# Four places in the order of one weighted cross attention stage, moved on TensorE, ScalarE, VectorE and GpSimd

## What is computed

```python
scores = jnp.einsum('bhqd,bhkd->bhqk', q, k) / jnp.sqrt(jnp.float32(d))   # 16 heads of 8
scores = scores * attention_weights            # (64, 16, 128, 77), read from memory
scores = jnp.where(attention_mask, -jnp.inf, scores)
p_attn = jax.nn.softmax(scores, axis=-1)
out = jnp.einsum('bhqk,bhkd->bhqd', p_attn, v)
out = out.transpose(0, 2, 1, 3).reshape(B, Nq, D) @ Wo.T + bo
x = queries + out                              # then layer norm, gamma, beta
```

## Time and profile before

| what | value |
|---|---|
| time, median of 3 runs | 2415.65 us (2414.92 to 2417.21) |
| time of the profiled execution | 2419.09 us |
| its span | 2417.3 us |
| granted TensorE clock, mean | 0.981 |
| busy, whole span: PE, DVE, ACT, POOL | 93%, 77%, 62%, 65% |
| A1, in the trace | from about 505 to 910 us |

### The profile page before, as it was taken

How to read it: one execution, slowest core, us unless ns; L and a number is a source line. 1 busy time by engine, 2 the same in 40 slices (tenths; PEclk the granted TensorE clock), 3 DMA queues, 4 the chain that set the end, 5 groups by cost and what they waited for, 6 DMA issues and landing times.

```text
span 2417.3 us, 90082 instructions
## 1 busy us (share of the span) xinstructions
PE 2249.4 (93%) x30214; PEld 1876.4 (78%) x30214; DVE 1862.4 (77%) x4063; ACT 1495.6 (62%) x3472; POOL 1567.2 (65%) x2374
## 2 busy tenths in 40 slices
PE   7999999978888888999999989999999999999799
PEld 5777778966666666777778968888888888888688
DVE  4888881159999996777775678899999999998465
ACT  5888885558888886888885524444444444444343
POOL 2666663139999994666667766666666666666333
PEclk9999999979999998999999989999999999999999
DMA  4111112245555542222221223333333333333121
GB/s 131 45 44 44 45 49 66 68 121 166 169 167 168 164 138 49 52 51 51 51 55 55 68 74 92 95 96 96 96 96 96 97 96 97 95 96 95 53 63 54
DMA packets 443731, 211.95 MB, mean 88 GB/s; under 512 B 206704, under 2 KB 434545, under 8 KB 443505
## 3 DMA queue, kind: packets, MB, share of 16 engines
q1 hardware_dynamic: 443632, 210.69, 32.5%
HBM read 113.54 MB, written 29.88 MB: 59 GB/s over the span
## 4 chain that ended last, share of the span: by engine, by line
PE 55%; POOL 16%; issue 12%; SPq 8%; DVE 4%; ACT 3%; DMA 1%; POOLq 0%; DVEq 0%; ACTq 0%
PE bank L1179 6%; PE bank L1453 6%; PE bank L701 5%; PE bank L1540 5%; PE bank L661 5%; PE bank L1193 4%; POOL sb_region L1038 4%; PE bank L721 3%; POOL sb_rstd L1055 3%; PE bank L1493 3%; SPq L1399 3%; SPq L1402 3%; POOL sb_z L1059 3%; PE bank L1479 2%; PE bank L1517 2%
## 5 line engine op out<-in xcount | busy, mean ns | idle before, releaser
L1739 POOL TENSOR_TENSOR sb_pn<-sb_l,sb_r_all 128x512 f32<-128x512 f32 x128 | 134.8, 1053 | 269.7 <-DVE sb_r_all L1670 228.0
L892 DVE TENSOR_REDUCE sb_max<-bank 128x8 f32<-128x616 f32 x256 | 203.3, 794 | 136.6 <-PE bank L675 69.5
L701 PE MATMUL bank<-sb_ident,sb_region 128*77 128x128 f32 x2048 | 274.5, 277 | 33.5 <-ACT sb_pT L798 32.2
L785 ACT ACTIVATE sb_region<-sb_region 128x616 f32<-128x616 f32 x384 | 276.0, 719 | 22.3 <-POOL sb_region L1038 20.8
L798 ACT ACTIVATE sb_pT<-bank 77x1024 f32<-77x1024 f32 x256 | 261.0, 1020 | 41.9 <-PE bank L701 41.8
L701 PEld LDWEIGHTS bank<-sb_ident,sb_region 128*77 128x77 f32 x2048 | 236.7, 152 | 62.1 <-issue 42.5
L897 DVE TENSOR_TENSOR sb_region<-bank,sb_max 128x616 f32<-128x616 f32 x256 | 204.6, 799 | 18.3
L721 PE MATMUL bank<-sb_pT,sb_v 77*32 77x128 f32 x6144 | 208.8, 276 | 2.8 <-ACT sb_pT L798 2.1
L721 PEld LDWEIGHTS bank<-sb_pT,sb_v 77*32 77x32 f32 x6144 | 155.6, 109 | 71.2 <-issue 65.1
L661 PE MATMUL bank<-sb_region,sb_qT 32*128 32x308 f32 x1536 | 158.8, 483 | 54.5 <-ACT sb_region L813 21.8
L1595 ACT ACTIVATE sb_oT<-bank 128x512 f32<-128x512 f32 x128 | 76.5, 598 | 213.9 <-PE bank L1507 213.9
(11 more groups left out here) (186 smaller groups left out, 6455.9 us busy)
## 6 DMA issues: line engine op xcount, KB each, us to landing
sb_region<-in_side SPq DMA_DIRECT2D x64, 616.0 KB, 3.8
sb_pT<-sb_region SPq DMA_DIRECT2D x512, 64.0 KB, 2.0
sb_kF<-sb_region SPq DMA_DIRECT2D x512, 64.0 KB, 2.1
scratch_after_A<-sb_y SPq DMA_DIRECT2D x256, 64.0 KB, 1.7
sb_fx<-scratch_after_A SPq DMA_DIRECT2D x96, 128.0 KB, 2.1
sb_mask<-in_mask SPq DMA_DIRECT2D x64, 154.0 KB, 2.3
sb_x<-scratch_after_F SPq DMA_DIRECT2D x128, 64.0 KB, 1.9
sb_ctx<-in_ctxT SPq DMA_DIRECT2D x192, 38.5 KB, 1.9
```

The source lines that it names most:

```text
L701: mm = nc.tensor.transpose(two[0:C, h * T:(h + 1) * T], p_s[b.par][:, head * C:(head + 1) * C], ident[:])
L785: nc.scalar.activation(half(p_s[b.par], k), half(p_s[b.par], k), ACT.Exp, scale=SCALE[ph]).then_inc(exp_made.sem(b), 1)
L892: nc.vector.tensor_reduce(dst, by_bank_and_head(scores_half(k)), AX.X, ALU.max).then_inc(max_made.sem(b), 1)
```

## The change

It changes only the order of calls within a step, in A1 only; A0 and A2 keep theirs. Nothing is computed otherwise, and no instruction or transfer is added or removed. On PE `attend(b-1, 1)` goes behind `transpose_p(b, 0)`. On ACT `keep_oT(b-2)` goes ahead of `keep_att(b-1)`. On DVE `peak_masked(b+1, 0)` goes ahead of `invert(b-1)`. On POOL `shift(b+1, 0)` goes ahead of `centre(b-3)`.

```diff
@@ PE, step
                 if has(-1):
                     attend(b + -1, 0, b + 2 if has(2) else None)
+                if has(-1) and ph != "A1":
                     attend(b + -1, 1)
                 if has(-2) and ph != "A0":
                     transpose_o(b + -2)
                 if has(0):
                     transpose_p(b, 0)
+                if has(-1) and ph == "A1":
+                    attend(b + -1, 1)
                 if has(-1):
                     back(b + -1)
@@ ACT, step
                 weighted = ph == "A1"
+                if has(-2) and weighted:
+                    keep_oT(b + -2)
                 if has(-1):
                     keep_att(b + -1)
-                if has(-2) and ph != "A0":
+                if has(-2) and ph == "A2":
                     keep_oT(b + -2)
@@ DVE, step_weighted
                 if has(1):
                     mask(b + 1, 0)
-                if has(-1):
-                    invert(b + -1)
                 if has(1):
                     peak_masked(b + 1, 0)
                 if has(-1):
+                    invert(b + -1)
                     normalise(b + -1)
@@ POOL, step
                     if has(-1):
                         residual(b + -1)
+                    if has(1):
+                        shift(b + 1, 0)
                     if has(-3):
                         centre(b + -3)
-                    if has(1):
-                        shift(b + 1, 0)
                     if has(-3):
                         affine(b + -3)
```

## The result

The changed kernel takes 2461.80 us (median of 3 runs, 2454.57 to 2462.11) against 2415.65 us: ratio 1.0186, 95% interval 1.0164 to 1.0209, 46 us more. The forecast was 2468 us, in a range of 2450 to 2478. The profiled execution took 2461.80 us; its span is 2460.0 us against 2417.3.

The account below looks back on a forecast made before the run. POOL with DVE's data was taken to set A1's 6.13 us step; a new loop of 4.79 + 0.28 + 0.13 + 1.00 + 0.80 = 7.00 us would add 52 us to 2415.65, giving 2468 us, range 2450 to 2478.

Parts of the forecast that it names:

- The loop and its place: In A1, last exponent, transposes, second attend, copy and ACT's step form a closed cycle of 7.00 us, against 6.13.
- Its links: Five parts of A1's new step: ACT's work 4.79, copy 0.28, wait 0.13, transposes to attend 1.00, attend to copy 0.80 us.
- exponent end to the start of the transposes: Wait in A1 between ACT's last exponent and PE's transposes of P, taken as 0.13 us.
- attend to copy: In A1, from the second attend's start on PE to its copy's start on ACT: 0.80 us, other bound 0.71.
- 0.2 us short of mattering: PE's other path, keep_q through scores and attend to transposes: 1.65 us, against 1.84 for the exponent's path.
- The ends: First copy in A1 late by 1 us; about 12 steps outside the program loop take back some 2 us.
- The other moves cost and bring nothing: In A1, reordering DVE, POOL and ACT was to have no effect; DVE and POOL have 1.2 us to spare.
- the only real gain: keep_oT ahead of the copy on ACT fills 0.16 to 0.28 us of its wait, already counted in the sum.
- The first rival: POOL stays A1's bound and its new order removes its idle time: 20 us less, 2396 us; chance 0.04.
- The shorter loop: Rival: every part of A1's closed cycle at its lower bound, 6.70 us a step, 35 us more, 2451 us.
- that rival: TensorE's clock falls in A1, lengthening each step by some 1.4 us: 85 us more, 2553 us; chance 0.02.
- The change does nothing: Rival: ACT's 0.47 us wait in A1 absorbs the new path, time within 0.2%, 2411 to 2420 us; chance 0.02.

Follow-up runs that it names:

- the order with the masks together: Kernel before, with DVE's mask of half 1 moved directly behind the mask of half 0: 2401.25 us, ratio 0.9949.

## Why the prediction was right, point by point

**The loop and its place.** Right, shown by the PE move alone (+58 us), by its removal (the loop gone), and by the extra operations: +10 us for 0.16 us a step on ACT, +2 us for 0.46 us a step on POOL.

**Its links.** Forecast 4.79 + 0.28 + 0.13 + 1.00 + 0.80 = 7.00 us; measured 4.75 + 0.28 + 0.05 + 1.03 + 0.79 = 6.90 in the round shown, and 4.76 + 0.28 + 0.07 + 1.03 + 0.77 = 6.91 on average over the 52 steps inside the program's loop. The mechanism was right and the sizes were each off by a few hundredths. The largest of these errors is "exponent end to the start of the transposes": I took the 0.15 us of a wait behind another copy, and it is 0.05 in 39 of the 52 steps and 0.13 or more in 13. The kernel before had shown the short value inside the loop too, where transposes follow the end of their copy (703.94) by 0.05:

```profile
702.94 1.00 ACT L798 ACTIVATE sb_pT<-bank 77x1024 f32<-77x1024 f32 x1
...
703.99 1.10 PE L701 MATMUL bank<-sb_ident,sb_region 128*77 128x128 f32 x8 [0.21 <-ACT sb_pT L798]
```

The link "attend to copy" is mixed as well, 0.79 us in 39 steps and 0.71 in 13. The 0.09 us of the sum, 52 times, is 4.7 us, most of the 6 us between 52 and 46.

**The path that was "0.2 us short of mattering".** PE's own queue up to the transposes came nearer than that, within 0.1 us of the exponent. As the extra ACT operation shows, the exponent is still the link that counts. Had ACT's work behind `keep_q` been 0.1 us shorter, the loop would by these rows have closed over the scores and the first attend instead; that is an estimate.

**The ends.** I put +1 us for the first copy and -2 for written-out steps. The first copy starts 17.90 us after A1's first matmul (504.86), where it started 17.25 us after it (506.64): +0.65. The written-out steps are 6.83 us long instead of 6.91 and the last 6.67, about 1 us together and not 2. The 61 steps grew by 46.6 us; the two spans differ by 42.7. Most of what lies between was there outside A1: A1 was reached 1.8 us earlier, and the program after the last copy of A1 took 1505.2 us instead of 1507.7. That code is the same in all fourteen traces and takes 1503.1 to 1507.7 us in them, so 2.5 us is within its spread, and the agreement of 46 us with 46.6 is in part luck.

**"The other moves cost and bring nothing."** Nearly true for the changed kernel, where the loop hides them and they take 2.8 us off. Not true in general, and this is the weak place of the text: I costed the POOL and DVE moves by DVE's and POOL's spare time and did not ask what the moved operations would then overlap. By themselves they cost 24 and 18 us. The forecast held because 7 us a step covered them. POOL's share in A1 fell to 89% and not to the 83% forecast, for the same reason: its centring takes 1404 ns (801 before).

**keep_oT.** I called it the only real gain, already in the sum. Added to the PE move alone it is worth 8 us, 0.13 us a step; in three steps of four it is 0.17 (7.08 against 6.91 us), and in the fourth the next exponent ends 0.19 us late, which takes it back.

**The first rival (POOL pays, 2396 us).** It failed twice: the loop covers it, and without the loop POOL's new order costs 24 us instead of giving 20. The Trainium skill ("Perfetto Trace Analysis", Identifying the Most-Contended Engine) says to optimise the engine with the highest occupancy first. The runs agree for the kernel before: the order with the masks together relieves POOL and is 13 us faster. They do not for the changed kernel: POOL is the fullest engine there too, at 89%, and one more POOL operation in each step costs 2 us.

**The others.** The shorter loop would have been 2451 us; its 0.05 held in three steps of four and its 0.71 in one of four, and the rest of it (0.88 from the transposes to the attend) never, that link being 0.98 to 1.03. The clock was 1.00 from 540 us on with PE at 82% by its rows, not the 74% forecast, so that rival had no footing. At A1's start it is 0.50 in both kernels, until about 522 us before and 518 after. The pause that this follows lies at the end of F0, ahead of A1: in the kernel before, PE was busy 2.29 of 5 us between 490 and 495 us, and from 495 us on the clock was 0.50. "The change does nothing" is excluded by the interval.

## What to carry to other kernels

When an operation is moved behind another on one engine, write down what the second waits for, and follow the chain until it comes back to the same engine: if it does, the length of that loop is the new least step, whatever the busy shares say, and it can be added up from the starts of rows in the profile of before. An engine that idles inside such a loop has no room, and an engine that is 89% busy outside it has. Where two engines exclude each other, a move must also be checked for what the moved operation then runs beside.

## What the runs showed of the hardware

DVE's mask (both tensor operands in SBUF) and POOL's operations take turns. A POOL operation that starts while the mask runs ends a nearly fixed time after the mask: the centring 0.67 us in the changed kernel and with the POOL move alone, the shift 1.07 to 1.08 us in the kernel before and with the DVE move alone, the root 0.42 to 0.43 us in all of these kernels (all rows between 540 and 900 us). A mask that starts while a shift runs ends 0.65 to 0.66 us after it and takes up to 1.50 us instead of 0.79 with the POOL move alone. DVE's product of scores (PSUM) and weights (SBUF) ran beside the same shifts without either changing: two of them take 1.51 us at 706.58 in the changed kernel while the shift of 706.85 keeps its 1.22. The Trainium skill ("GPSIMD Engine Reference", 1. Specifications) says that GpSimd shares its SBUF interfaces with VectorE and contends with its instructions that have two SBUF inputs; the traces agree.

One overlap stays open. In the kernel before the centring begins 0.33 to 0.49 us ahead of a mask, overlaps it for the rest of its 0.80 us, and costs neither of them anything. In the changed kernel, in one step of four, it begins only 0.13 us ahead and gives way all the same:

```profile
711.05 1.59 POOL L1063 TENSOR_SCALAR sb_z<-sb_t,sb_mv,sb_rstd 128x128 f32<-128x128 f32 x1
...
711.18 0.79 DVE L915 SCALAR_TENSOR_TENSOR sb_region<-sb_mask,sb_region 128x616 f32<-128x616 uint8 x1
```

So neither the start of a POOL row nor its length tells the stretch in which it excludes the mask.
